# The scan's products of state and output row, in the third layer's attention, on VectorE instead of GpSimd

## The reference

```
q = rmsnorm(LN(x) @ Wq, gq);  k = rmsnorm(ctx @ Wk, gk);  v = ctx @ Wv
out = softmax(q k^T / sqrt(128)) v, per head;   x += tanh(g) * (out @ Wo)
```

```
state = state * exp(delta_t * A) + (delta_t * u_t) * B_t     # per channel and state
y_t   = sum over states of state * C_t
y     = (y + D * u) * silu(LN(x))
```

## Time and profile before

| | |
|---|---|
| median of 3 runs | 1503.24 us (1495.06 to 1506.06) |
| profiled execution | 1501.21 us |
| its span | 1499.5 us |
| TensorE busy | 1157.1 us (77%) |
| VectorE busy | 912.9 us (61%) |
| ScalarE busy | 625.2 us (42%) |
| GpSimd busy | 601.0 us (40%) |
| the product L497 on POOL | 32 times, 75.1 us busy |
| the product L497 on DVE (second layer) | 32 times |

### The profile page before, as it was taken

How to read it: one execution, slowest core, us unless ns; L and a number is a source line. 1 busy time by engine, 2 the same in 40 slices (tenths; PEclk the granted TensorE clock), 3 DMA queues, 4 the chain that set the end, 5 groups by cost and what they waited for, 6 DMA issues and landing times.

```text
span 1499.5 us, 18673 instructions
## 1 busy us (share of the span) xinstructions
PE 1157.1 (77%) x5364; PEld 877.2 (59%) x5365; DVE 912.9 (61%) x1614; ACT 625.2 (42%) x1680; POOL 601.0 (40%) x369
## 2 busy tenths in 40 slices
PE   6756587676357867798898889868999943999993
PEld 3445476565124545576677677646555533888772
DVE  4578798776538963888888887882322357232222
ACT  4481454434242115666675666744111113333231
POOL 1007588888301112434434344330000000788884
PEclk9786799888659889999999999988999956899997
DMA  5815799886400001120220221014500099455555
GB/s 160 164 8 139 204 289 290 212 228 136 109 26 1 0 29 36 43 71 8 78 78 1 77 77 49 23 36 146 155 1 0 0 250 230 89 79 81 80 80 123
DMA packets 130071, 145.62 MB, mean 97 GB/s; under 512 B 29510, under 2 KB 114239, under 8 KB 129991
## 3 DMA queue, kind: packets, MB, share of 16 engines
q1 hardware_dynamic: 105414, 111.10, 25.4%
q0 software_dynamic: 24576, 33.57, 13.6%
HBM read 118.52 MB, written 26.12 MB: 96 GB/s over the span
## 4 chain that ended last, share of the span: by engine, by line
PE 31%; issue 21%; DVE 15%; POOL 14%; DMA 9%; ACT 5%; SPq 5%; DVEq 0%; POOLq 0%; ACTq 0%
PE bank L1873 5%; DMA f_sums<-arena,put 4%; PE bank L1459 3%; POOL f_sums L889 3%; PE bank L2167 3%; PE bank L1882 3%; DVE arena L477 2%; SPq L2052 2%; POOL arena L875 2%; POOL y L2089 2%; ACT arena L1596 2%; PE bank L1420 2%; DVE ssm_part L518 2%; PE bank L1477 2%; DVE x_top L1654 2%
## 5 line engine op out<-in xcount | busy, mean ns | idle before, releaser
L477 DVE TENSOR_TENSOR_SCAN arena<-arena 128x1024 f32<-128x1024 f32 x64 | 146.3, 2286 | 28.0 <-issue 22.4
L497 POOL TENSOR_TENSOR arena<-arena 128x1024 f32<-128x1024 f32 x32 | 75.1, 2346 | 178.1 <-DVE arena L477 178.1
L889 POOL DMA_INDIRECT f_sums<-arena,put x64 | 133.1, 2079 | 24.9 <-issue 15.6
L202 POOL TENSOR_TENSOR rstd<-var_eps,minus_half 128x8 f32<-128x8 f32 x8 | 13.7, 1708 | 290.1 <-DVE var_eps L192 290.1
L875 POOL DMA_INDIRECT arena<-y_rows,slots x64 | 91.8, 1434 | 84.8 <-DVEq L1082 58.7
L1596 ACT ACTIVATE arena<-bank,x_nb,x_rq 128x256 f32<-128x256 f32 x128 | 71.1, 559 | 104.8 <-DVE x_nb L1658 104.8
L2167 PE MATMUL bank<-arena,ssm_y 128*128 x512 | 111.7, 362 | 3.6 <-ACT ssm_y L2235 2.2
L455 ACT ACTIVATE arena<-arena,ssm_A 128x255 f32<-128x255 f32 (+1 forms) x256 | 108.1, 499 | 7.9 <-DVE arena L430 7.9
L2079 POOL DMA_INDIRECT e_sums<-ctxT,put x64 | 101.7, 1588 | 23.8 <-issue 16.7
L1873 PE MATMUL bank<-yT,arena 128*128 128x512 f32 (+1 forms) x224 | 103.7, 607 | 0.0
L2089 POOL DMA_INDIRECT y<-y_rows,slots x64 | 67.5, 1054 | 73.6 <-DMA y_rows<-y 54.3
(11 more groups left out here) (307 smaller groups left out, 2727.9 us busy)
## 6 DMA issues: line engine op xcount, KB each, us to landing
arena<-bc_rows SPq DMA_DIRECT2D x64, 512.0 KB, 5.8
arena<-in_L_ffn_w_gate_dram SPq DMA_DIRECT2D x32, 256.0 KB, 3.5
arena<-in_L_ffn_w_up_dram SPq DMA_DIRECT2D x32, 256.0 KB, 4.2
arena<-in_L_ffn_w_down_dram SPq DMA_DIRECT2D x32, 256.0 KB, 5.7
arena<-in_L_ffn_Wd_dram SPq DMA_DIRECT2D x1, 3072.0 KB, 24.2
f_sums<-arena SPq DMA_DIRECT2D x2, 1024.0 KB, 5.9
y_rows<-y SPq DMA_DIRECT2D x2, 1024.0 KB, 10.9
arena<-f_sums SPq DMA_DIRECT2D x8, 256.0 KB, 5.8
```

What stands on the lines that cost most here:

```text
L477: nc.vector.tensor_tensor_scan(ssm_h[:, j % 2, :], ssm_decay[:, j % 2, :], ssm_in, 0.0, ALU.mult, ALU.add).then_inc(s_ssm_h, 1)
L889: nc.gpsimd.indirect_dma_start(out=f0_sums[m % SUMS], out_offset=bass.IndirectOffsetOnAxis(ap=put[:, m:m + 1], axis=0), in_=f0_ye[:, n % R ...
```

## The change

In an odd step of the attention DVE issues the product of state and output row directly behind its scan; the two products of a head are taken out of POOL's queue. The function `ssm_hC` is the same for both engines: it issues its three waits and the multiplication on the engine that it is given.

```
@@ -1691,6 +1691,7 @@
                 j = 2 * k + b // 2
                 if par:
                     ssm_scan(dve, 1, i, j)
+                    ssm_hC(dve, nc.vector, 1, i, j)
                 elif j:
                     ssm_reduce_dve(dve, 1, i, j - 1)
                 elif not first:
@@ -1732,11 +1733,9 @@
 
             def head(i, k, final=False):
                 h = i * HB + k
-                ssm_hC(pool, nc.gpsimd, 1, i, 2 * k)
                 if not final:
                     rms(h + 1, (k + 1) % 2)
                     qrms(h + 1, (k + 1) % 2)
-                ssm_hC(pool, nc.gpsimd, 1, i, 2 * k + 1)
 
             rms(0, 0)
             qrms(0, 0)
```

## The result

The changed kernel takes 1540.42 us (median of 3 runs, 1537.53 to 1542.64) against 1503.24 before: 37.2 us more, ratio 1.0257 with a 95% interval of 1.0204 to 1.0310. It is slower, by more than the 28 us forecast: inside the stated range of 1518 to 1545, but above the 1524 to 1538 of the main forecast, where the prediction had placed its two dearer rivals. The profiled execution took 1537.53 us with a span of 1535.8.

What follows compares the result with a forecast made beforehand. DVE, with its round trip through ACT, was taken to lead, PE following. Terms 2.5 + 7.2 + 15.6 + 2.5 = 27.8, say 28 us, gave a median of 1531 us; range 1518 to 1545.

Steps and rivals of the forecast that it cites:

- two dearer rivals: PE's clock falling in even heads too (1543 us, chance 0.17); product and power blocking each other (1539 to 1543, 0.13).
- Price of one product: Each product behind a scan on DVE: 3.47 us from scan to next instruction instead of 2.20, costing 1.27 us.
- Site a: First scan of an even head: the following row maximum comes later, PE slips; cost 1.05 us, 1.25 in the loop.
- Site b: Second scan of an even head: the next head's row maximum, whose rows PE awaits, comes 1.27 us later.
- Site c: First scan of an odd head: nothing absorbs the product; cost 1.27 us, 1.37 in the loop.
- Site d: Second scan of an odd head: DVE idles for POOL's `x_rq` anyway; cost 0, other end 1.5 us.
- End of the stage: Last sum over states, behind the final scan: starts earlier without waiting for POOL's product, gain 1.1 us.
- PE's clock: Rival: PE idles before even heads' key transposes, its clock falls there; +9 to +17 us, taken +12; chance 0.17.
- Signs: In the trace: products 1.22 us, row maxima 3.47 us after scans at a, b, c, pair 56.9 us, PE busy unchanged.
- PE in DVE's place: Rival: PE's queue sets the pace, DVE's delay vanishes; 1502 us, half absorbed 1517; chance 0.10 for full or mostly absorbed.
- Shut out: Rival at site d: DVE's product and POOL's power block each other; 8 to 12 us, 1539 to 1543; chance 0.13.
- loop surcharge: Heads 4 to 11, register-counted loop: waits cost 0.2 us more at a, half at c, 0.3 a pair.

Runs made afterwards that it cites:

- site b alone: Kernel before with only the second product of each even head moved from POOL to DVE; ratio 1.0084 (1.0043 to 1.0126).
- site d alone: Kernel before with only the second product of each odd head moved from POOL to DVE; ratio 1.0006 (0.9970 to 1.0042).
- the earlier variance: Kernel before with the queries' variance prepared ahead of the copy of the values in step 3, so POOL's power starts before the scan; ratio 0.9911.

## Why the prediction was right, and where its size was off

Direction and mechanism held: the product lengthens DVE's path at three sites of four, and POOL's freedom is worth nothing. By its own steps:

- *Price of one product* (1.27 us): 1.26 at b and c, 1.25 at a. Right. The extra 0.1 to 0.2 us for the waits in the loop was wrong: c has 1.26 in and out of the loop, a 1.25 to 1.35.
- *Site a* (1.05, in the loop 1.25): 1.25 to 1.35 less 0.28 in the next step, 1.0 us. Right in kind and size.
- *Site b* (1.27): the base line is 1.32. Right.
- *Site c* (1.27): 1.26. Right.
- *Site d* (0): -0.4 to +0.2 alone, +1.8 us in all in the changed kernel. Right, and the product is not held beside the power, as the rows with scan and power had said. The range's other end, 1.5 us each, did not occur.
- *End of the stage* (gain of 1.1 us): the sum starts 1.16 us earlier behind its scan. Right.
- *PE's clock.* This is the term that was mis-sized. The sum had it at zero, and a rival with 0.17 had it at +12 us. Measured in the profiled run: 3 x 1.7 = 5 us in even heads, where the rival placed it, and 4 x 1.3 = 5 us in step 1 of odd heads, which the prediction had not named. There PE waits for the rows of step 0, 2.36 us in head 3 of the changed kernel against 1.02 in that head before, and then runs slowly; site b alone did the same. The rival's price of a fallen clock, 1.2 to 2.5 us per head, held (1.7), but in three heads of seven.
- *Signs.* Products 1.22 us long, row maxima 3.46 us after the scans at a to c and 3.9 at d, longer waits of PE and a power of 3.46 us at d all came. PE's busy time did not stay unchanged (49.16 us in the pair instead of 46.27), and products of the same site in the loop stand 58.3 to 59.9 us apart, not 56.9: both go with the lower clock. The sign against it, even heads' transposes of twice 1.07 us, came in one head of seven (1.97 us in head 10, 1.50 in head 8, 1.09 in the others).
- *Rivals.* PE in DVE's place: absorbed 0.28 us in seven steps, no more. Shut out: gone, by site d alone and by the earlier variance. For a scan that starts while a power of 8 columns runs, the Trainium skill's rule (SBUF — State Buffer, "SBUF: two separate sides") of a block for the whole instruction did not hold (2.28 us as ever), nor for the product at d, if the power then ran; a scan that starts before the power does hold it (3.46 us instead of 1.64).

The sum's 27.8 us are 28.9 up to the last row maximum, since the gain of 1.1 lies behind it. Less the 1.2 of the loop surcharge, plus 10.1 for the clock and 1.8 at d they make 39.6, against 40.2 measured; the rest of the kernel ran 3.9 us shorter in that execution, 1 us of which is the end of the stage. So the sum of a right path was about 11 us short in the stage, and the time lies within the range because that reached up to the two dearer rivals. What stays open is in which heads the clock falls: step 1 of two or three even heads was 1.7 us longer with only site c or d moved, where nothing is changed, so part of the 10 us may belong to the particular execution.

## What to carry to other kernels

Before moving work to a faster engine, ask where on that engine's path it will stand: the same 32 instructions cost 37 us behind the scans and nothing in a wait one step later. Price the added idle time of TensorE too, not only the added work of the engine that sets the pace, because behind a longer wait its clock can be lower, and that comes back as a wait of the first engine. And where a step costs nothing because a stall covers it, look at the stall: removing it made the kernel before 13 us faster, while the best placement of the product only made it cost nothing.

## What the runs showed of the hardware that I had not expected

POOL's power on 8 columns and DVE's instructions with two SBUF inputs don't hold each other alike. Started 0.2 us before the scan, the power takes 1.64 us and the scan 2.28; started 0.25 us after the scan's start, it ends 3.46 us later, and a product that begins 2.06 us after it was issued takes 1.22 us as ever. POOL's scaling of the keys (128 x 1024) does hold a DVE addition that starts during it, 2.07 us instead of 0.42, as the earlier trace rows had it before the change. The two at 865 us, in the changed kernel, DVE first:

```profile
865.39 2.07 DVE L522 TENSOR_TENSOR ssm_y<-ssm_y,ssm_part 128x256 f32 x1
```

```profile
865.29 1.89 POOL L1726 TENSOR_TENSOR arena<-arena,x_rk 128x1024 f32<-128x1024 f32 x1
```
